# Three-layer TAGConv with LayerNorm: 46 input tiles transposed by DMA from fp16 halves instead of on PE

## The reference

```python
def _tagconv(x, src, dst, norm, W, b):
    out = x @ W[0]
    h = x
    for k in range(1, K + 1):
        msg = norm[:, None] * h[src]
        h = jax.ops.segment_sum(msg, dst, num_segments=x.shape[0])
        out = out + h @ W[k]
    return out + b

h = jax.nn.relu(_tagconv(x, src, dst, norm, W1, b1))
h = jax.nn.relu(_tagconv(h, src, dst, norm, W2, b2))
x = _layernorm(x + _tagconv(h, src, dst, norm, W3, b3))
```

## Time and profile before

| what | value |
|---|---|
| median of 3 runs | 1280.93 us (1280.33 to 1280.96) |
| the profiled execution | 1280.98 us, of which the span of instructions is 1279.2 us |
| PE busy | 1242.9 us, 97% of the span |
| DVE, ACT, POOL busy | 635.3, 358.9, 835.1 us |
| granted PE clock | 0.995 of full, so the 2.4 GHz level |
| DMA engines, mean busy share | 41%: 30.6% for the gathers, 10.2% for what SP issues |

### The profile page before, as it was taken

One profiled execution on the slowest core, in us unless ns is written; L12 is line 12 of the kernel. 1 busy time (PEld: TensorE's weight loads), 2 busy tenths in 40 slices (PEclk: granted clock), 3 DMA queues, 4 the chain that ended last, 5 costly groups with the idle time before them and its releaser, 6 DMA issues.

```text
span 1279.2 us, 19722 instructions
## 1 busy us (share of the span) xinstructions
PE 1242.9 (97%) x7539; PEld 626.0 (49%) x7539; DVE 635.3 (50%) x1622; ACT 358.9 (28%) x863; POOL 835.1 (65%) x927
## 2 busy tenths in 40 slices
PE   4899999999999999999999999999999999999997
PEld 3555554444554554444544455554444544454443
DVE  6986662444445455443443345545433433345655
ACT  4866663221122222111221112222111111112222
POOL 7476554777477672777577747763677577747773
PEclk9999998999999999999999999999999999999999
DMA  5333333454334342444354424432444344435552
GB/s 167 103 113 99 95 98 90 141 143 132 89 113 131 110 124 75 129 135 130 102 154 136 128 80 124 131 111 80 120 132 130 99 129 131 130 93 148 155 161 85
DMA packets 86908, 152.76 MB, mean 119 GB/s; under 512 B 18488, under 2 KB 60119, under 8 KB 86808
## 3 DMA queue, kind: packets, MB, share of 16 engines
q0 software_dynamic: 40048, 109.36, 30.6%
q1 hardware_dynamic: 46760, 42.08, 10.2%
HBM read 119.26 MB, written 32.10 MB: 118 GB/s over the span
## 4 chain that ended last, share of the span: by engine, by line
PE 92%; DVE 5%; POOL 1%; issue 1%; ACT 1%; DMA 0%; DVEq 0%; POOLq 0%
PE pb L1184 68%; PE pb L1085 9%; PE pb L1087 4%; PE pb L1113 4%; PE pb L1004 2%; PE pb L1189 1%; PE pb L1162 1%; DVE pb L1526 1%; POOL GB L847 1%; PE pb L1134 1%; DVE V L1497 1%; DVE gT L1475 1%; DMA gT<-in_table,idx 0%; DVE V L1289 0%; DVE Whl L1370 0%
## 5 line engine op out<-in xcount | busy, mean ns | idle before, releaser
L847 POOL DMA_INDIRECT GB<-vh,KS x828 | 795.6, 961 | 411.3 <-issue 242.2
L1184 PE MATMUL pb<-V,A 128*128 128x512 f16 x4104 | 936.5, 380 | 0.0
L1184 PEld LDWEIGHTS pb<-V,A 128*128 128x128 fp8e4 x4104 | 397.0, 98 | 442.2 <-issue 2.1
L1526 DVE SCALAR_TENSOR_TENSOR pb<-pb,cst,t 128x256 f32<-128x256 f32 (+1 forms) x225 | 109.9, 489 | 358.7 <-ACT t L970 358.7
L970 ACT ACTIVATE t<-pb,cst 128x256 f32<-128x256 f32 (+1 forms) x250 | 118.1, 473 | 495.7 <-PE pb L1189 424.6
L1085 PE MATMUL pb<-Whl,gT 128*128 128x512 f16 x576 | 204.0, 382 | 2.1 <-DVE gT L1475 1.5
L1087 PE MATMUL pb<-Whl,gT 128*128 128x256 f16 x576 | 157.6, 274 | 0.0
L1497 DVE SCALAR_TENSOR_TENSOR V<-V,pb 128x256 f16<-128x256 f16 (+1 forms) x225 | 94.1, 420 | 92.7 <-ACT V L944 92.0
L944 ACT ACTIVATE V<-pb 128x256 f16<-128x256 f32 (+1 forms) x225 | 85.5, 382 | 132.0 <-DVE pb L1526 131.9
L1085 PEld LDWEIGHTS pb<-Whl,gT 128*128 128x128 f16 x576 | 56.4, 98 | 78.9 <-issue 20.8
L1391 DVE TENSOR_REDUCE stat<-V 128x1 f32<-128x256 f16 x225 | 91.3, 412 | 0.2
(11 more groups left out here) (195 smaller groups left out, 547.5 us busy)
## 6 DMA issues: line engine op xcount, KB each, us to landing
vh<-V SPq DMA_DIRECT2D x216, 128.0 KB
GB<-vh,KS POOLq DMA_INDIRECT x828, 2.8
xr<-in_x SPq DMA_DIRECT2D x24, 128.0 KB, 2.9
out<-g SPq DMA_DIRECT2D x24, 128.0 KB, 1.9
xr<-in_W SPq DMA_DIRECT2D x16, 128.0 KB, 3.0
V<-in_x SPq DMA_DIRECT2D x4, 384.0 KB, 6.5
V<-in_x SPq DMA_DIRECT2D x3, 512.0 KB, 5.0
V<-in_W SPq DMA_DIRECT2D x2, 512.0 KB, 4.6
```

Source lines behind the costliest of these rows:

```text
L847: pool.indirect_dma_start(GB[:, slot, :], None, vh[vbuf[(L, k + 1)]][:, :], bass.IndirectOffsetOnAxis(ap=KS[:, p:p + 1], axis=0))\
L1184: mm = pe.matmul(acc[:, :], A8[:, a, t * P:(t + 1) * P], src[:, a, :], start=False, stop=(n == NT - 1), skip_group_check=True)
L1526: dve.scalar_tensor_tensor(hi, hi, cst[0:r, 1, t:t + 1], lt, ALU.mult, ALU.add).then_inc(S["s_d1"], 1)
```

## The change

For the 23 tiles other than 18 and 23 of each LONG hop, the transposes leave PE.

- DVE writes g (node layout) as before. ACT then makes the high fp16 half from it, and DVE the low half, in `split[n % 2]`, which lies in the memory of `w[:, n % 2]`. So DVE waits for ACT within a tile's work, and ACT waits for DVE's g.
- SP issues one DMA transpose for the tile (`flip`): 128 rows of 512 fp16 values (128 KB) become the four 128 x 128 blocks of `gT[:, t]`. SP's stores of V for k = 3 now stand three places behind the flips (`LAG`).
- DVE waits before it writes `we` of place n until the flip of place n - 2 has landed, since both use `w[:, n % 2]`.
- PE waits for the landing, not for DVE's line 1475, before P(L+1, 3, t) of these tiles.
- ACT's line 935 and DVE's line 1475 go for these tiles, and with them a PSUM bank's turn. The range check reads `split`. Tiles 18 and 23 are done as before, from `g[:, 2 + j % 2]`.
- The first layer's input (L = 0) is transposed on PE as before.

```diff
+def by_queue(L, t):
+    return L > 0 and t not in (TD - 1, NT - 2)
...
+            def flip(L, t):
+                if by_queue(L, t):
+                    n = n_of[(L - 1, 0, t)]
+                    sp.wait_ge(S["s_xl"], x_no[(L, t)] + 1)
+                    sp.dma_start_transpose(gT[:, t].rearrange("p c h m -> p (c h) m"),
+                                           split[n % 2].rearrange("p c h m -> p (c h m)")).then_inc(s_xt[n % 2], 16)
...
+                if k == 3:
+                    for n in range(NT):
+                        flip(L, order[(L - 1, 0)][n])
+                        if n >= LAG:
+                            keep(L, k, n - LAG)
+                    for n in range(NT - LAG, NT):
+                        keep(L, k, n)
+                    continue
...
+                if k == 0 and by_queue(L + 1, t) and L < 2:
+                    n = n_of[(L, k, t)]
+                    act.wait_ge(S["s_xg"], x_no[(L + 1, t)] + 1)
+                    act.activation(split[n % 2][:, :, 0, :], g[:, n % 2, :].rearrange("p (c m) -> p c m", c=2),
+                                   ACT.Copy, scale=1.0 / SC).then_inc(S["s_xh"], 1)
...
-                if k == 3:
+                if k == 3 and by_queue(L, t):
+                    pe.wait_ge(s_xt[n_of[(L - 1, 0, t)] % 2], landings(L, t))
+                elif k == 3:
                     pe.wait_ge(S["s_tl"], t_no[(L, t)] + 1)
...
+                    if n > 1 and by_queue(L + 1, earlier):
+                        dve.wait_ge(s_xt[n % 2], landings(L + 1, earlier))
                     dve.scalar_tensor_tensor(we, hi, SC / SV, t2[0:r, n % 2, :], ALU.mult,
                                              ALU.add).then_inc(S["s_d1"], 1)
                     dve.wait_ge(S["s_d1"], e + 1)
-                    dve.wait_ge(S["s_tp"], j - RB + 1)
-                    dve.tensor_scalar(g[0:r, j % RB, :], we, 0.0, None, ALU.max).then_inc(S["s_g"], 1)
+                    if by_queue(L + 1, t):
+                        dve.wait_ge(S["s_tp"], NT)
+                        dve.tensor_scalar(g[0:r, n % 2, :], we, 0.0, None, ALU.max).then_inc(S["s_xg"], 1)
+                        dve.wait_ge(S["s_xh"], x_no[(L + 1, t)] + 1)
+                        dve.scalar_tensor_tensor(split[n % 2][:, :, 1, :], split[n % 2][:, :, 0, :], -SC,
+                                                 g[:, n % 2, :].rearrange("p (c m) -> p c m", c=2),
+                                                 ALU.mult, ALU.add).then_inc(S["s_xl"], 1)
+                        largest(9 * NT + turn_no[(L + 1, t)], split[n % 2][:, :, 0, :], AX.XY)
+                        continue
+                    j = t_no[(L + 1, t)]
+                    dve.wait_ge(S["s_tp"], j - 1)
+                    dve.tensor_scalar(g[0:r, 2 + j % 2, :], we, 0.0, None, ALU.max).then_inc(S["s_g"], 1)
```

More of the change, by code:

```diff
@@ L70 @@
 MEANWHILE = (6, 8, 14)
+LAG = 3
 LATER = (0, 2, 5, 9, 10, 15)
@@ L466, in bass_tag_gnn_layernorm @@
     SCHED = schedule()
-    pe_no, v_no, t_no = {}, {}, {}
+    pe_no, v_no, t_no, x_no, turn_no = {}, {}, {}, {}, {}
     n_of, free_of = {}, {}
@@ L471, in bass_tag_gnn_layernorm @@
         if it[0] == "T":
-            t_no[it[1:]] = len(t_no)
+            turn_no[it[1:]] = len(turn_no)
+            numbers = x_no if by_queue(*it[1:]) else t_no
+            numbers[it[1:]] = len(numbers)
         elif it[0] == "G":
@@ L596, in bass_tag_gnn_layernorm @@
                  "s_v s_gx s_g s_tp s_th s_tl s_z s_ln s_sd s_o s_dd s_st s_ck s_pk s_flag s_turn s_lp "
-                 "s_ld s_pl s_at s_at0 s_sg s_dl s_pc s_ps5 s_cp5 s_k5 s_t5 s_s5 s_gm s_nr s_wl").split()
+                 "s_ld s_pl s_at s_at0 s_sg s_dl s_pc s_xg s_xh s_xl s_ps5 s_cp5 s_k5 s_t5 s_s5 s_gm s_nr s_wl").split()
         S = {n: sem(n) for n in names}
@@ L600, in bass_tag_gnn_layernorm @@
         s_xl = [sem(f"s_xl{i}") for i in range(RB)]
+        s_xt = [sem(f"s_xt{i}") for i in range(2)]
         s_x = [sem(f"s_x{i}") for i in range(len(XC) - 1)]
@@ L606, in bass_tag_gnn_layernorm, with landings @@
         s_gb = [sem(f"s_gb{i}") for i in range(NSLOT)]
+        split = [w[:, i, :].bitcast(F16).rearrange("p (c h m) -> p c h m", c=2, h=2) for i in range(2)]
+        def landings(L, t):
+            return 16 * len([key for key, i in x_no.items()
+                             if i <= x_no[(L, t)] and n_of[(key[0] - 1, 0, key[1])] % 2 == n_of[(L - 1, 0, t)] % 2])
         block = ctx.enter_context(nc.Block())
@@ L1123, in work @@
                     _, L, t = it
+                    if by_queue(L, t):
+                        return
                     j = t_no[(L, t)]
@@ L1133, in work @@
                     for c in range(2):
-                        mm = pe.transpose(TB[j % 2][:, c * P:(c + 1) * P], g[:, j % RB, c * P:(c + 1) * P],
+                        at = j % RB if L == 0 else 2 + j % 2
+                        mm = pe.transpose(TB[j % 2][:, c * P:(c + 1) * P], g[:, at, c * P:(c + 1) * P],
                                           identf[:, :])
@@ L1478, in _ @@
                     if L:
-                        largest(9 * NT + j, gT[:, t, :, 0, :], AX.XY)
+                        largest(9 * NT + turn_no[(L, t)], gT[:, t, :, 0, :], AX.XY)
                     continue
@@ L1528, in _ @@
                 elif L < 2:
-                    j = t_no[(L + 1, t)]
+                    earlier = order[(L, 0)][n - 2] if n > 1 else 0
                     dve.wait_ge(S["s_a1"], e + 1)
```

## The result

| | before | after |
|---|---|---|
| median | 1280.66 us (6 runs, 1280.07 to 1281.22) | 1270.48 us (6 runs, 1268.96 to 1273.59) |
| ratio | | 0.9923, 95% interval 0.991 to 0.9935 |
| profiled execution, its span | 1280.98 us, 1279.2 us | 1268.96 us, 1267.2 us |

A forecast was written before the change was run, and what follows sets the result against it. PE, busy 97% of the span, was taken as the bound. Per LONG hop 4.84 + 0.72 = 5.56 us, both 11.1: 1280.98 - 11.1 = 1269.9 us, own range 1268.5 to 1271.3, full range 1268.0 to 1281.5.

The forecast's parts named there:

- PE's 0.22 us for each tile: PE's gapless stream: removing two transposes saves 0.22 us for each of 22 tiles, 4.84 us a LONG hop.
- The hop's end, 0.72 us: LONG hop's end: P(17)'s stall goes, P(18) still waits for DVE; 0.72 us gained, tile 17's 0.22 within it.
- The next hop starts in the same relation: Last stores into `vh`, which release POOL's next gathers, move with P(18) and P(23), so the hop's gain carries over.
- What hides the split: DVE waits about 0.5 us per tile for ACT, ACT about 1.4 for g; DVE's 72 idle us cover it, costing nothing.
- The flips, 3 to 5 us: DMA transposes land in 3 to 5 us, under limits of 7.8 at tile 17 and 6.8 at DVE, costing nothing.
- Rival (a): Flips hold gathers up on the DMA engines: PE stalls up to 4.8 us a hop at tile 19, 1274.7 to 1279.5; chance 0.17.
- Rival (b): Late flips stall PE at P(17) and DVE ahead of `we`: slower, 1299.3 us at a 10 us landing; chance 0.13.
- break-even of 9.2 us: Flip landing time at which PE's waits for late flips would reach the 5.56 us gained in a hop.
- the five places: DVE's wait ahead of `we` behind each of five gathered groups, limit 6.8 us, where a late flip delays the next.

The follow-up runs named there:

- pe_back: Changed kernel with two PE transposes of the identity, read by nobody, put back for each of the 46 tiles: 1280.02 us, ratio 0.9995.
- late_one_tile: Changed kernel with each flip issued only when PE has ended the next tile's last matmul: 1271.1 us, ratio 0.9924.
- flips_x2: Changed kernel with one more whole transpose of the same split half to spare memory behind each flip: 1269.08 us, ratio 0.9911.
- slack_after: Changed kernel with gathered tiles of the two hops that follow a LONG hop taken up one dense tile later: 1269.53 us, ratio 0.9913.
- after_again: Changed kernel unaltered, timed again beside other kernels on the same chip: 1270.59 us, ratio 0.992 to the kernel before.
- no_flip: Changed kernel without its 46 DMA transposes and the waits for them, so layers 2 and 3 get wrong input: 1269.64 us, ratio 0.9911.
- late_tile_and_flip: Changed kernel with each flip held until PE ended the next tile's last matmul and a transposed copy to spare memory landed: 1307.69 us, ratio 1.022.
- all_by_queue: Changed kernel with tiles 18 and 23 transposed by DMA as well: 1274.5 us, ratio 0.9957.

## Why the prediction was right

- **PE's 0.22 us for each tile**: shown. 4.84 us a hop from 22 tiles were predicted; pe_back, which gives all 23 back, costs 5.06 us in the first LONG hop, 23 x 0.22. The length of the transposes in the table, 280 ns, would have given 46 x 0.56 = 26 us.
- **The hop's end, 0.72 us**: right. From tile 17's last matmul to P(18) 0.93 us went, against the 0.94 of the steps (0.72, and 0.22 for the transposes of tile 16, which stand in that stretch too). P(17)'s stall went and P(18)'s became 0.44, within 0.3 to 0.7; pe_back shows the 0.5 us beyond tile 17's transposes by themselves. One hop was to give 5.56 us; measured at P(18) it gave 5.55 and 5.51.
- **The next hop starts in the same relation**: the one step that failed, by 0.1 us in the profile after and by some 2 us in others. It holds for the first hop (1.98 us from the write of V(23) to POOL's gather, as before). In the second it was 2.05 and 2.14 in the two profiles of the changed kernel (1.96 before), and 4.1 in late_one_tile, which differs from it only in flips that are issued later. The prediction took the landing of stores and gathers as fixed, where the traces show a 16 KB instruction packet ahead of the last eight packets of a late store, and nowhere asked how much room PE has at the first gathered tile of the next hop. It has almost none: a store 2.1 us behind its write cost PE 0.36 us there in flips_x2. That the median is 0.6 us above the forecast and the runs spread over 4.6 us fits this, and so does slack_after, with 1269.5 us and a spread of 0.9; one of these runs alone, after_again's, was followed to its cause.
- **How near the number is**: the two hops gave 11.06 us against 11.1, and that is the mechanism. That the median came within 0.6 us of 1269.9 is in part luck, as it depends on where in an execution those packets fall.
- **What hides the split**: right. 0.48 us of DVE and 1.47 of ACT for a tile, predicted 0.5 and 1.4; no_flip and pe_back show no cost of it on PE.
- **The flips, 3 to 5 us**: right in the hop, with a median of 3.35 us for the same transfer in late_tile_and_flip, and too long for the hop's end, 2.5. The issue of tile 17's flip came 3.18 us after its last matmul (473.77 to 476.95), predicted 3.0. The Trainium skill's 1309 ns by DMA in "VectorE: DVE Perf Modes", section "The three transpose paths", led to an estimate of 7.1 us for four blocks in series, and these numbers refute it. The Trainium skill's rule in the same page's "Rules for kernel authors", to transpose 128 x 128 on TensorE where PSUM will do, doesn't hold for this kernel, which PE bounds: it is 10.2 us faster by DMA. The Trainium skill's 261 GB/s in "DMA: Bandwidth & Descriptors", section "Latency and other measured facts", led to an estimate of 0.5 us for 128 KB, which holds only the moving; the flip of tile 23 in all_by_queue moved its packets in 0.8 us (490.35 to 491.12), and the other 1.8 of its 2.5 us are issue and completion.
- **Rival (a)**: refuted by flips_x2 up to a share of 0.68: landings of 2.8 us in the median and no wait of PE on `GB` in a LONG hop.
- **Rival (b)**: didn't happen, but its mechanism is real: in late_tile_and_flip DVE waits ahead of `we`, and flips and PE are late behind it, at 12.0 us of PE's waiting a hop. Its price and its break-even of 9.2 us are not shown, since the five places went from 3.4 us in late_one_tile to 8.1 and more with nothing between. What is shown as room in the change is 4.7 us of lateness at tile 17 and at dense tiles, and at the five places one more transpose behind each flip (flips_x2).

## What to carry to other kernels

Work that leaves the bounding engine pays by the distance from one start to the next in its stream, not by the length of its row, and a copy that replaces it is free as long as a whole tile of other work lies between its issue and its reader. Price the landing beside the transfers that will run with it (3.35 us here, not the 2.5 with nothing beside it), and look for a buffer that is used again two tiles on: there lateness feeds back, and flips 5 to 9 us late cost 37 us. After a gain, look at the next place with no room; with one dense tile moved ahead of the first gathered one, nine runs of two kernels kept within 1 us each.

## What the runs showed of the hardware

- A transpose of 128 x 512 fp16 from SBUF to SBUF by DMA takes SP 1.20 us to issue and lands 2.5 us after the issue starts while nothing else moves (all_by_queue), 3.35 us in the median beside gathers, 5.3 at most (late_tile_and_flip). 23 of them in 140 us raise the DMA engines' share from 0.39 to 0.52.
- Gathers of 128 KB keep their median landing of 2.8 us with these transposes beside them up to a DMA share of 0.68, and 2.9 at 0.73; single ones take 4.8 and more.
- The store of V(23) lands 1.96 to 2.0 us after its write in most hops and 3.5 to 4.3 in some, at a DMA share of about 0.2. In each late case a 16 KB packet of the kind "instruction" of 1.0 to 1.6 us ran in between, with the store's last eight packets of 1 KB right behind it.
- Of 13 stalls of PE between 0.4 and 3.4 us in late_tile_and_flip, five (1.87 to 2.87 us) were followed by a granted clock of half for some 3 us, and eight weren't, the longest among them. The one at 429.49 cost 1.4 us on top of its wait: 1.2 in the projections, 0.2 in the 24 matmuls behind them. In after_again a wait of 2.12 us was followed by the same.
